# LoRA kernel on one core: A read as 128 rows of 4 KB in one transfer, its table columns put in place by the copies out of PSUM

## The chip, the cores and the metric

The kernel runs on one core of one Trainium2 chip. The metric is the device time in microseconds; the time of the kernel before is the median of three runs, 93.06 us (93.05 to 93.09).

## What is computed

Each of 64 sequences (64 tokens of 1024 features, float32) names one of 8 adapters of rank 16. The low-rank product of that adapter is added to the sequence:

```python
B_sel = B[adapter_ids]                       # B: [8, 16, 1024]
A_sel = A[adapter_ids]                       # A: [8, 1024, 16]
Bx = jnp.einsum('bni,bri->bnr', x, B_sel)
out = jnp.einsum('bnr,bor->bno', Bx, A_sel)
x = x + out * SCALING                        # SCALING = 1
```

x is 16 MB in and 16 MB out; A and B are 512 KB each.

## The kernel before

**Tiling.** x is 32 tiles of 128 tokens (two sequences each), all of which fit in SBUF (`x_all`). Two tiles make a duo, and the steady loop goes over 16 duos. For each duo TensorE transposes the eight 128x128 blocks of each tile (L217), multiplies them with the rank rows of B (`down`, L228) and, one duo later, multiplies the small result with the columns of A (`up`, L248). ScalarE copies the transposed x out of PSUM (`copy_x`, L301) and makes the high part of the small result (L316, L283); VectorE makes the remaining part (L352) and adds the product onto x (`add_x`, L361). GpSimd fetches the rows of the adapter that each sequence names from `b_table` (L156) and `a_table` (L166).

**Setup.** Before that the two tables are made. B is loaded by ScalarE's queue and transposed (L192), and two ScalarE copies write `b_table` (L293). A is loaded by SP's queue in two transfers of 256 KB, four adapters each. Partition p gets 8 successive outputs of each adapter, which are 512 contiguous bytes in HBM. A is split into a part that holds the high bits and a rest, in four pairs of adapters: ScalarE casts (L289), VectorE subtracts (L340). TensorE then transposes one adapter in four matmuls (`a_unit`, L206), each of which writes every fourth column of half a PSUM tile, so that the columns come out in order and a plain 512-element copy moves one adapter into `a_table`: six of the eight copies are VectorE's (L345), units 5 and 7 are ScalarE's (L306). The units take turns in four PSUM banks, so units 4 to 7 wait for the copies of units 0 to 3. TensorE runs 21 warm-up transposes on the identity first (L187). Its order is then: B, A units 0 to 3, the transposes of tile 0, A units 4 and 5, the transposes of tile 1, A units 6 and 7, the loop.

**Transfers.** SP issues, in this order on one queue: the A transfers, 17 loads of x (two of 512 KB, 15 of 1 MB), then the 32 stores of 512 KB, each when `add_x` of its tile is done. The loads that overwrite the place of A and its parts (tiles 26 to 31) wait for `a_filled`. Nothing but the last wait reads `stored`.

Of the kernel before, what the change touches and what calls it, by code (L numbers as in the profile page):

```python
# [8 lines left out]
def lora_kernel(nc: bass.Bass, x: bass.AP, ids: bass.AP, a_in: bass.AP, b_in: bass.AP, out: bass.AP):  # L9
# [5 lines left out]
    P = 128  # L15
# [16 lines left out]
    B_HOME, A_HOME, PARTS_HOME = TILES - 1, TILES - 2, TILES - 6  # L32
    B_OWN = CHUNKS * RANK
    WARM_UPS = 21
    GROUP = ADAPTERS // 2
    PAIR = 2
    PAIRS = ADAPTERS // PAIR

    rows = x.rearrange("s t d -> (s t) d").rearrange("(n p) d -> p n d", p=P)
    out_rows = out.rearrange("s t d -> (s t) d").rearrange("(n p) d -> p n d", p=P)  # L40
# [5 lines left out]
    with ctx:  # L46
# [6 lines left out]
        def sem(name):  # L53
# [10 lines left out]
        a_duo = [sb(f"a_duo{i}", [P, DUO_SEQS, BANK], F32R) for i in range(2)]  # L64

        b_nat = x_all[:, B_HOME, :]
        a_nat = x_all[:, A_HOME, :].rearrange("p (a o) -> p a o", a=ADAPTERS)
        a_parts = (x_all[:, PARTS_HOME:A_HOME, :].rearrange("p n d -> p (n d)")
                   .rearrange("p (a j k) -> p a j k", a=ADAPTERS, j=J))

        t_bank = [pb(f"t_bank{i}", [P, BANK]) for i in range(2)]
        bx_bank = [pb(f"bx_bank{i}", [P, BANK]) for i in range(2)]
        y_banks = [pb(f"y_banks{i}", [P, D]) for i in range(2)]

        ids_loaded = sem("ids_loaded")
        a_loaded = [sem(f"a_loaded{g}") for g in range(2)]
        b_loaded = sem("b_loaded")
        x_loaded = [sem(f"x_loaded{n}") for n in range(len(LOADS))]
        stored = sem("stored")
# [21 lines left out]
            half = a % A_BANKS // 2  # L101
            return y_banks[a % 2][:, half * BANK:(half + 1) * BANK]

        def a_raw(pair):
            raw = a_nat[:, pair * PAIR:(pair + 1) * PAIR, :].rearrange("p a (o r) -> p (a o) r", r=RANK)
            return raw.unsqueeze(2).to_broadcast([P, PAIR * J * HALVES, 2, RANK])

        def a_part(pair, part):
            both = (a_parts[:, pair * PAIR:(pair + 1) * PAIR, :, :]
                    .rearrange("p a j (h e t r) -> p (a j h) e t r", h=HALVES, e=2, t=2))  # L110
            return both[:, :, :, part, :]

        def a_row(a):
            return a_table[:, a * BANK:(a + 1) * BANK]

        def own_tokens(duo, first_row, end_row):
            blocks = (bx_parts[duo % 2][first_row:end_row, :, :]
# [2 lines left out]

        @block.sync
        def _(sp):
            for g in range(2):
                of = slice(g * GROUP, (g + 1) * GROUP)
                sp.dma_start(a_nat[:, of, :],
                             a_in.rearrange("a (p o) r -> p a (o r)", p=P)[:, of, :]).then_inc(a_loaded[g], 16)
            for n, (first, end) in enumerate(LOADS):
                if end > PARTS_HOME:
                    sp.wait_ge(a_filled, ADAPTERS)
                sp.dma_start(x_all[:, first:end, :], rows[:, first:end, :]).then_inc(x_loaded[n], 16)  # L130
            for tile in range(TILES):
                sp.wait_ge(y_drained, tile + 1)
                sp.dma_start(out_rows[:, tile, :], x_all[:, tile, :]).then_inc(stored, 16)
            sp.wait_ge(stored, 16 * TILES)
# [48 lines left out]
        @block.tensor  # L183
        def _(pe):
            pe.wait_ge(ident_steps, 2)
            for _ in range(WARM_UPS):
                nc.tensor.transpose(t_bank[0][:, 0:P], ident[:, :], ident[:, :])  # L187

            pe.wait_ge(b_loaded, 16)
            for unit in range(B_UNITS):  # L190
                for c in range(HALF):
                    last = nc.tensor.transpose(bx_bank[unit][:, c * P:(c + 1) * P],  # L192
                                               b_nat[:, (unit * HALF + c) * P:(unit * HALF + c + 1) * P], ident[:, :])
                last.then_inc(t_filled, 1)

            def a_unit(a):
                if a % PAIR == 0:
                    pe.wait_ge(a_rest_done, a // PAIR + 1)
                before = a - A_BANKS
                if before in A_BY_ACT:  # L200
                    pe.wait_ge(a_copied_act, A_BY_ACT.index(before) + 1)
                if before in A_BY_DVE:
                    pe.wait_ge(a_copied_dve, A_BY_DVE.index(before) + 1)
                filled = a_bank(a).rearrange("k (p j) -> k p j", j=J)
                for j in range(J):
                    last = nc.tensor.transpose(filled[:, :, j], a_parts[:, a, j, :], ident[:, :])  # L206
                last.then_inc(a_filled, 1)

            def transpose_unit(duo, unit):
                tile, half = unit // 2, unit % 2  # L210
                if unit == 0 or duo == 0 and half == 0:
                    pe.wait_ge(x_loaded[LOAD_OF[2 * duo + tile]], 16)
                if duo or unit >= 2:
                    pe.wait_ge(t_copied, B_UNITS + UNITS * duo + unit - 1)
                for c in range(HALF):
                    at = (half * HALF + c) * P
                    last = nc.tensor.transpose(t_bank[unit % 2][:, c * P:(c + 1) * P],  # L217
                                               x_all[:, 2 * duo + tile, at:at + P], ident[:, :])
                last.then_inc(t_filled, 1)

            def down(duo, first, end):
                if first == 0:
                    pe.wait_ge(b_gathered, duo + 1)
                pe.wait_ge(t_copied, B_UNITS + UNITS * duo + (3 if end <= HALF else 4))
                for c in range(first, end):
                    for k in range(DUO_SEQS):
                        tile, s = k // PER_TILE, k % PER_TILE
                        last = nc.tensor.matmul(bx_bank[duo % 2][k * QUAD:(k + 1) * QUAD, 0:SEQ],  # L228
                                                b_duo[duo % 2][:, k, c, :],
                                                x_t[duo % 2][:, c, tile, s * SEQ:(s + 1) * SEQ],  # L230
                                                start=(c == 0), stop=(c == CHUNKS - 1))
                if end == CHUNKS:
                    last.then_inc(bx_done, 1)

            def up(duo):
                pe.wait_ge(a_gathered, duo + 1)
                pe.wait_ge(parts_done, duo + 1)
                for tile in range(2):
                    if duo == 0:
                        pe.wait_ge(a_copied_act, len(A_BY_ACT))  # L240
                        pe.wait_ge(a_copied_dve, len(A_BY_DVE))
                    else:
                        pe.wait_ge(y_drained, 2 * (duo - 1) + tile + 1)
                    for s in range(PER_TILE):
                        for h in range(HALVES):
                            ranks = slice(h * K_UP, (h + 1) * K_UP)
                            k = tile * PER_TILE + s
                            last = nc.tensor.matmul(y_banks[tile][:, h * BANK:(h + 1) * BANK],  # L248
                                                    bx_parts[duo % 2][ranks, k, :], a_duo[duo % 2][ranks, k, :],
                                                    start=(s == 0), stop=(s == PER_TILE - 1))  # L250
                    last.then_inc(y_filled, 1)

            for a in range(A_BANKS):
                a_unit(a)
            transpose_unit(0, 0)
            transpose_unit(0, 1)
            a_unit(A_BANKS)
            a_unit(A_BANKS + 1)
            transpose_unit(0, 2)
            transpose_unit(0, 3)  # L260
            a_unit(A_BANKS + 2)
            a_unit(A_BANKS + 3)
            for duo in range(DUOS):
                if duo + 1 < DUOS:
                    transpose_unit(duo + 1, 0)
                    transpose_unit(duo + 1, 1)
                down(duo, 0, HALF)
                if duo + 1 < DUOS:
                    transpose_unit(duo + 1, 2)
                    transpose_unit(duo + 1, 3)  # L270
                down(duo, HALF, CHUNKS)
                if duo:
                    up(duo - 1)
            up(DUOS - 1)

        @block.scalar
        def _(act):
# [5 lines left out]
                nc.scalar.copy(own_tokens(duo, K_UP, 2 * K_UP),  # L283
                               own_tokens(duo, 0, K_UP)).then_inc(parts_done, 1)

            for pair in range(PAIRS):
                if pair % 2 == 0:
                    act.wait_ge(a_loaded[pair // 2], 16)
                nc.scalar.copy(a_part(pair, 0).bitcast(F32R), a_raw(pair)).then_inc(a_high_done, 1)  # L289

            for unit in range(B_UNITS):
                act.wait_ge(t_filled, unit + 1)
# [10 lines left out]

            def copy_a(a):
                act.wait_ge(a_filled, a + 1)
                nc.scalar.copy(a_row(a), a_bank(a)).then_inc(a_copied_act, 1)  # L306

            def split_high(duo):
                act.wait_ge(bx_done, duo + 1)
# [25 lines left out]

        @block.vector
        def _(dve):
            for pair in range(PAIRS):
                dve.wait_ge(a_high_done, pair + 1)
                nc.vector.tensor_tensor(a_part(pair, 1).bitcast(F32R), a_raw(pair), a_part(pair, 0),  # L340
                                        ALU.subtract).then_inc(a_rest_done, 1)

            for a in A_BY_DVE:
                dve.wait_ge(a_filled, a + 1)
                nc.vector.tensor_copy(a_row(a), a_bank(a)).then_inc(a_copied_dve, 1)  # L345

            def split_rest(duo):
                dve.wait_ge(high_done, duo + 1)
# [37 lines left out]
```

## Time and profile before

| | |
|---|---|
| median of 3 runs | 93.06 us |
| the profiled execution | 93.04 us, of which the span from the first to the last instruction is 91.2 us |
| TensorE busy (matmul / weight load) | 80.1 / 63.0 us |
| VectorE, ScalarE, GpSimd busy | 59.7, 59.0, 60.3 us |
| moved by DMA | 34.82 MB, mean 382 GB/s |
| mean granted TensorE clock | 0.961 |

In the profile "PE" is TensorE's matmuls, "PEld" its weight loads, DVE is VectorE, ACT ScalarE, POOL GpSimd. "L206" is line 206 of the kernel, shown above. A DMA share of 1.0 means that all 16 DMA engines of the core are moving packets; 0.06 is one of them.

### The profile page before, as it was taken

The numbers are of one execution on the slowest core, as the hardware profiler recorded it, in microseconds if no ns is written. First come the engines' busy times: TensorE is split into PE (matmuls) and PEld (weight loads), VectorE is DVE, ScalarE is ACT, GpSimd is POOL, SyncE is SP. The second block draws the span as 40 slices with busy tenths as digits, with TensorE's granted clock in tenths as the row PEclk, the third lists the DMA queues.
The fourth block names the chain that finished last, engine by engine and source line by source line (L and its number), as shares of the span: only waits on it lengthen the run. The fifth ranks groups of instructions, "written<-read, shape, count | busy, mean of one in ns | idle before, by whom it ended". The sixth has DMA issues, their size and how long they took to land.

```text
span 91.2 us, 3627 instructions
## 1 busy us (share of the span) xinstructions
PE 80.1 (88%) x1469; PEld 63.0 (69%) x1469; DVE 59.7 (65%) x106; ACT 59.0 (65%) x153; POOL 60.3 (66%) x136
## 2 busy tenths in 40 slices
PE   3999999999999999899999999999999999464400
PEld 3999988778687778587778687878787786322100
DVE  0039930359686768775959586776869696999900
ACT  1367698969696859396869596969695958131000
POOL 6000859999879697877878879797979793900000
PEclk9999999999999999999999999999999999999555
DMA  1899999999999999999999999999999999988890
GB/s 25 311 386 410 408 410 412 401 413 410 395 413 408 404 412 403 406 412 403 410 412 404 415 419 408 412 415 410 422 408 413 430 397 421 392 345 356 341 386 20
DMA packets 10193, 34.82 MB, mean 382 GB/s; under 512 B 834, under 2 KB 1858, under 8 KB 10178
## 3 DMA queue, kind: packets, MB, share of 16 engines
q1 hardware_dynamic: 10032, 34.08, 93.7%
q10 hardware_dynamic: 146, 0.52, 1.5%
q8 instruction: 11, 0.18, 0.8%
q14 instruction: 4, 0.03, 0.1%
HBM read 17.83 MB, written 16.78 MB: 380 GB/s over the span
## 4 chain that ended last, share of the span: by engine, by line
PE 85%; DVE 6%; issue 1%; ACT 1%; POOL 1%; POOLq 0%
PE t_bank L217 36%; PE y_banks L248 20%; PE bx_bank L228 20%; PE t_bank L187 5%; DVE x_all L361 4%; PE y_banks L206 4%; DVE bx_parts L352 2%; PE bx_bank L192 1%; ACT bx_parts L283 1%; POOL ident L140 0%; POOL ident L138 0%; POOLq L140 0%; POOLq L377 0%
## 5 line engine op out<-in xcount | busy, mean ns | idle before, releaser
L361 DVE TENSOR_TENSOR x_all<-y_banks,x_all 128x1024 f32<-128x1024 f32 x32 | 39.4, 1232 | 15.7 <-PE y_banks L248 15.1
L301 ACT COPY x_t<-t_bank 128x512 f32<-128x512 f32 x64 | 34.5, 592 | 13.9 <-PE t_bank L217 13.3
L166 POOL CAST a_duo<-a_table 128x512 fp32r x64 | 36.7, 615 | 3.1 <-PE y_banks L248 2.1
L217 PE MATMUL t_bank<-ident,x_all 128*128 128x128 f32 x256 | 34.9, 279 | 0.0
L156 POOL COPY b_duo<-b_table 128x256 f32 x64 | 22.8, 401 | 15.8 <-PE bx_bank L228 8.7
L217 PEld LDWEIGHTS t_bank<-ident,x_all 128*128 128x128 f32 x256 | 27.5, 141 | 7.0 <-issue 5.4
L248 PE MATMUL y_banks<-a_duo,bx_parts 64*128 64x512 f32 x128 | 20.6, 429 | 3.6 <-ACT bx_parts L283 3.2
L228 PE MATMUL bx_bank<-x_t,b_duo 128*32 128x64 f32 x1024 | 21.3, 222 | 0.0
L228 PEld LDWEIGHTS bx_bank<-x_t,b_duo 128*32 128x32 f32 x1024 | 16.1, 109 | 5.6 <-issue 5.2
L352 DVE TENSOR_TENSOR bx_parts<-bx_bank,bx_parts 32x64 fp32r<-32x64 f32 x64 | 14.1, 220 | 4.8 <-ACT bx_parts L316 3.7
L248 PEld LDWEIGHTS y_banks<-a_duo,bx_parts 64*128 64x128 f32 x128 | 10.9, 188 | 7.3 <-issue 3.8
L316 ACT CAST bx_parts<-bx_bank 32x64 fp32r<-32x64 f32 x64 | 13.1, 205 | 0.9 <-PE bx_bank L228 0.2
L283 ACT CAST bx_parts<-bx_parts 64x256 fp32r<-64x256 f32 x16 | 6.5, 405 | 5.3 <-DVE bx_parts L352 4.2
L340 DVE TENSOR_TENSOR x_all<-x_all 128x512 fp32r<-128x512 f32 x4 | 2.5, 688 | 6.0 <-ACT x_all L289 6.0
L187 PE MATMUL t_bank<-ident 128*128 128x128 f32 x21 | 4.4, 404 | 1.5 <-POOL ident L140 1.5
L187 PEld LDWEIGHTS t_bank<-ident 128*128 128x128 f32 x21 | 4.2, 221 | 1.5 <-POOL ident L140 1.5
L206 PE MATMUL y_banks<-ident,x_all 128*128 128x128 f32 x32 | 4.0, 274 | 0.0
L345 DVE CAST a_table<-y_banks 128x512 fp32r<-128x512 f32 x6 | 3.8, 685 | 0.3 <-PE y_banks L206 0.3
L206 PEld LDWEIGHTS y_banks<-ident,x_all 128*128 128x128 f32 x32 | 3.5, 140 | 0.2 <-DVE x_all L340 0.2
L289 ACT CAST x_all<-x_all 128x512 fp32r<-128x512 f32 x4 | 2.2, 616 | 2.2 <-DMA x_all<-in_A 2.2
L289 ACT ACT_TABLE_LOAD x1 | 1.3, 1283 | 1.9 <-issue 1.9
L306 ACT CAST a_table<-y_banks 128x512 fp32r<-128x512 f32 x2 | 1.1, 612 | 0.0
(10 smaller groups left out, 4.9 us busy)
## 6 DMA issues: line engine op xcount, KB each, us to landing
out_y<-x_all SPq DMA_DIRECT2D x32, 512.0 KB, 13.2
x_all<-in_x SPq DMA_DIRECT2D x15, 1024.0 KB, 19.0
x_all<-in_x SPq DMA_DIRECT2D x2, 512.0 KB, 6.1
x_all<-in_B ACTq DMA_DIRECT2D x1, 512.0 KB, 4.3
x_all<-in_A SPq DMA_DIRECT2D x2, 256.0 KB, 4.8
id_row<-in_ids ACTq DMA_DIRECT2D x1, 0.2 KB
```

Source lines behind the costliest of these rows:

```text
L156: last = nc.gpsimd.tensor_copy(b_duo[duo % 2][:, k, :, :].rearrange("p c (e r) -> p c e r", e=2), b_table[:, bass.ds(adapters[k] * B_OWN, ...
L166: last = nc.gpsimd.tensor_copy(a_duo[duo % 2][:, k, :], a_table[:, bass.ds(adapters[k] * BANK, BANK)])
L187: nc.tensor.transpose(t_bank[0][:, 0:P], ident[:, :], ident[:, :])
L206: last = nc.tensor.transpose(filled[:, :, j], a_parts[:, a, j, :], ident[:, :])
L217: last = nc.tensor.transpose(t_bank[unit % 2][:, c * P:(c + 1) * P], x_all[:, 2 * duo + tile, at:at + P], ident[:, :])
L228: last = nc.tensor.matmul(bx_bank[duo % 2][k * QUAD:(k + 1) * QUAD, 0:SEQ], b_duo[duo % 2][:, k, c, :], x_t[duo % 2][:, c, tile, s * SEQ:( ...
L248: last = nc.tensor.matmul(y_banks[tile][:, h * BANK:(h + 1) * BANK], bx_parts[duo % 2][ranks, k, :], a_duo[duo % 2][ranks, k, :], start=(s ...
L283: nc.scalar.copy(own_tokens(duo, K_UP, 2 * K_UP), own_tokens(duo, 0, K_UP)).then_inc(parts_done, 1)
L301: nc.scalar.copy(x_t[duo % 2][:, half * HALF:(half + 1) * HALF, tile, :], t_bank[unit % 2][:, :].rearrange("p (c n) -> p c n", c=HALF)).th ...
L316: last = nc.scalar.copy(bx_parts[duo % 2][0:QUAD, k, s * SEQ:(s + 1) * SEQ], bx_bank[duo % 2][k * QUAD:(k + 1) * QUAD, 0:SEQ])
L352: last = nc.vector.tensor_tensor(bx_parts[duo % 2][QUAD:K_UP, k, cols], bx_bank[duo % 2][k * QUAD:(k + 1) * QUAD, 0:SEQ], bx_parts[duo % 2 ...
L361: nc.vector.tensor_tensor(here, product, here, ALU.add).then_inc(y_drained, 1)
```

## The change

A is read in one transfer of 128 rows of 4 KB: partition 16a + b holds outputs 64b to 64b + 63 of adapter a. The split into the two parts keeps its four instructions on each engine (now over quarters of the row). A transpose of 128 columns now gives one pair of outputs (l of 0 to 31) for all adapters and blocks, and writes 128 neighbouring PSUM columns. Each of the eight copies out of PSUM still moves 512 elements on each of 128 partitions, but reads four columns that stand 128 apart (512 bytes) and writes them as a run of four (16 bytes), with 128 such runs, one in every 32 columns of `a_table`. The table's content is as before. The core of the diff:

```diff
         def _(sp):
-            for g in range(2):
-                of = slice(g * GROUP, (g + 1) * GROUP)
-                sp.dma_start(a_nat[:, of, :],
-                             a_in.rearrange("a (p o) r -> p a (o r)", p=P)[:, of, :]).then_inc(a_loaded[g], 16)
+            sp.dma_start(a_nat, a_in.rearrange("a (b o) r -> (a b) (o r)", b=BLOCKS)).then_inc(a_loaded, 16)
...
-                filled = a_bank(a).rearrange("k (p j) -> k p j", j=J)
                 for j in range(J):
-                    last = nc.tensor.transpose(filled[:, :, j], a_parts[:, a, j, :], ident[:, :])
+                    last = nc.tensor.transpose(a_bank(a)[:, j * P:(j + 1) * P], a_parts[:, a * J + j, :], ident[:, :])
...
-            for pair in range(PAIRS):
-                if pair % 2 == 0:
-                    act.wait_ge(a_loaded[pair // 2], 16)
-                nc.scalar.copy(a_part(pair, 0).bitcast(F32R), a_raw(pair)).then_inc(a_high_done, 1)
+            for quarter in range(QUARTERS):
+                if quarter == 0:
+                    act.wait_ge(a_loaded, 16)
+                nc.scalar.copy(a_part(quarter, 0).bitcast(F32R), a_raw(quarter)).then_inc(a_high_done, 1)
...
-        def a_row(a):
-            return a_table[:, a * BANK:(a + 1) * BANK]
+        def a_columns(u):
+            return (a_table[:, :].rearrange("k (a b l) -> k a b l", a=ADAPTERS, b=BLOCKS)
+                    [:, :, :, u * J:(u + 1) * J])
+
+        def a_filled_columns(u):
+            return a_bank(u).rearrange("k (l a b) -> k a b l", l=J, a=ADAPTERS)
...
-                nc.scalar.copy(a_row(a), a_bank(a)).then_inc(a_copied_act, 1)
+                nc.scalar.copy(a_columns(a), a_filled_columns(a)).then_inc(a_copied_act, 1)
...
-                nc.vector.tensor_copy(a_row(a), a_bank(a)).then_inc(a_copied_dve, 1)
+                nc.vector.tensor_copy(a_columns(a), a_filled_columns(a)).then_inc(a_copied_dve, 1)
```

## Rows read from the trace of the kernel before

**Rows 1.** The page: span, the two DMA rows of the 40 slices, the chain by line.

```profile
span 91.2 us, 3627 instructions
...
DMA  1899999999999999999999999999999999988890
GB/s 25 311 386 410 408 410 412 401 413 410 395 413 408 404 412 403 406 412 403 410 412 404 415 419 408 412 415 410 422 408 413 430 397 421 392 345 356 341 386 20
...
PE t_bank L217 36%; PE y_banks L248 20%; PE bx_bank L228 20%; PE t_bank L187 5%; DVE x_all L361 4%; PE y_banks L206 4%; DVE bx_parts L352 2%; PE bx_bank L192 1%; ACT bx_parts L283 1%; POOL ident L140 0%; POOL ident L138 0%; POOLq L140 0%; P
```

**Rows 2.** Busy time by engine, clock and DMA in stretches of the end.

```profile
48.50:77.00 28.50, 28.50 (x586) 22.27 (x576) 21.60 (x39) 22.33 (x61) 23.27 (x51) 1.00 1.03 414
...
80.70:81.40 0.70, 0.62 (x4) 0.18 (x4) 0.70 (x1) 0.00 (x0) 0.00 (x0) 1.00 0.62 252
...
84.10:84.80 0.70, 0.70 (x4) 0.47 (x4) 0.70 (x1) 0.00 (x0) 0.00 (x0) 0.50 0.24 99
85.00:88.70 3.70, 0.29 (x2) 0.00 (x0) 1.51 (x2) 0.00 (x0) 0.00 (x0) 0.50 1.01 411
88.90:89.10 0.20, 0.00 (x0) 0.00 (x0) 0.00 (x0) 0.00 (x0) 0.00 (x0) 0.50 0.21 82
89.30:90.30 1.00, 0.00 (x0) 0.00 (x0) 0.00 (x0) 0.00 (x0) 0.00 (x0) 0.50 0.06 25
```

**Rows 3.** Line L133: the last store (issued at 86.6 us), and all stores.

```profile
L133 SPq DMA_DIRECT2D out_y<-x_all x1: 332/332/332, 86.6 to 86.6; - x1
DMA to landing us min/median/max: 4.2/4.2/4.2
...
L133 SPq DMA_DIRECT2D out_y<-x_all x32: 332/383/2969, 32.8 to 86.6; - x32
DMA to landing us min/median/max: 3.8/13.2/16.5
```

**Rows 4.** DMA queues over the whole span: packets, MB, share.

```profile
q8 instruction: 11, 0.18, 0.8%
```

**Rows 5.** Timeline of the setup: start, us, engine, line, tiles.

```profile
0.74 0.99 SPq L125 DMA_DIRECT2D x_all<-in_A  x2
...
5.38 2.18 ACT L289 CAST x_all<-x_all 128x512 fp32r<-128x512 f32 x4 [2.22 <-DMA x_all<-in_A]
5.68 0.90 PEld L192 LDWEIGHTS bx_bank<-ident,x_all 128*128 128x128 f32 x8
...
6.78 1.73 PEld L206 LDWEIGHTS y_banks<-ident,x_all 128*128 128x128 f32 x16 [0.20 <-DVE x_all L340]
...
8.45 3.08 DVE L345 CAST a_table<-y_banks 128x512 fp32r<-128x512 f32 x5
...
11.10 0.90 PEld L206 LDWEIGHTS y_banks<-ident,x_all 128*128 128x128 f32 x8
...
12.88 1.12 ACT L301 COPY x_t<-t_bank 128x512 f32<-128x512 f32 x2
...
13.63 0.86 PEld L217 LDWEIGHTS t_bank<-ident,x_all 128*128 128x128 f32 x8
```

**Rows 6.** Busy time by engine, clock, DMA share and GB/s in stretches of the start.

```profile
1.80:2.50 0.70, 0.70 (x5) 0.70 (x5) 0.00 (x0) 0.63 (x1) 0.60 (x2) 1.00 0.41 97
2.50:3.00 0.50, 0.50 (x4) 0.50 (x3) 0.00 (x0) 0.50 (x1) 0.00 (x0) 1.00 0.68 242
3.00:4.00 1.00, 1.00 (x7) 1.00 (x6) 0.00 (x0) 0.15 (x1) 0.00 (x0) 1.00 1.03 400
4.00:5.00 1.00, 1.00 (x7) 1.00 (x6) 0.00 (x0) 0.00 (x0) 0.00 (x0) 1.00 1.04 331
5.00:5.60 0.60, 0.60 (x5) 0.60 (x5) 0.00 (x0) 0.22 (x1) 0.00 (x0) 1.00 1.28 399
5.60:15.00 9.40, 9.40 (x132) 8.78 (x134) 6.18 (x10) 7.83 (x16) 4.61 (x12) 1.00 1.02 408
```

**Rows 7.** DMA queues in the stretch 3.5 to 4.4 us: q1 is SP's, q10 ACT's.

```profile
q10 hardware_dynamic: 76, 0.26, 72.2%
q1 hardware_dynamic: 149, 0.08, 27.9%
```

**Rows 8.** Groups by line and shape: busy, mean ns of one, idle before.

```profile
L361 DVE TENSOR_TENSOR x_all<-y_banks,x_all 128x1024 f32<-128x1024 f32 x32 | 39.4, 1232 | 15.7 <-PE y_banks L248 15.1
...
L217 PE MATMUL t_bank<-ident,x_all 128*128 128x128 f32 x256 | 34.9, 279 | 0.0
...
L206 PE MATMUL y_banks<-ident,x_all 128*128 128x128 f32 x32 | 4.0, 274 | 0.0
L345 DVE CAST a_table<-y_banks 128x512 fp32r<-128x512 f32 x6 | 3.8, 685 | 0.3 <-PE y_banks L206 0.3
...
L306 ACT CAST a_table<-y_banks 128x512 fp32r<-128x512 f32 x2 | 1.1, 612 | 0.0
```

More of the change, by code:

```diff
@@ L34, in lora_kernel @@
     WARM_UPS = 21
-    GROUP = ADAPTERS // 2
-    PAIR = 2
-    PAIRS = ADAPTERS // PAIR
+    BLOCKS = P // ADAPTERS
+    A_UNITS = 8
+    QUARTERS = 4
+    PER_QUARTER = A_UNITS * J // QUARTERS
     rows = x.rearrange("s t d -> (s t) d").rearrange("(n p) d -> p n d", p=P)
@@ L66, in lora_kernel @@
         b_nat = x_all[:, B_HOME, :]
-        a_nat = x_all[:, A_HOME, :].rearrange("p (a o) -> p a o", a=ADAPTERS)
+        a_nat = x_all[:, A_HOME, :]
         a_parts = (x_all[:, PARTS_HOME:A_HOME, :].rearrange("p n d -> p (n d)")
-                   .rearrange("p (a j k) -> p a j k", a=ADAPTERS, j=J))
+                   .rearrange("p (l k) -> p l k", k=P))
         t_bank = [pb(f"t_bank{i}", [P, BANK]) for i in range(2)]
@@ L75, in lora_kernel @@
         ids_loaded = sem("ids_loaded")
-        a_loaded = [sem(f"a_loaded{g}") for g in range(2)]
+        a_loaded = sem("a_loaded")
         b_loaded = sem("b_loaded")
@@ L102, in a_bank, with a_raw, a_part @@
             return y_banks[a % 2][:, half * BANK:(half + 1) * BANK]
[L104 to L110, printed above, removed]
-            return both[:, :, :, part, :]
-        def a_row(a):
-            return a_table[:, a * BANK:(a + 1) * BANK]
+        def a_raw(quarter):
+            size = PER_QUARTER * HALVES
+            raw = a_nat[:, quarter * size * RANK:(quarter + 1) * size * RANK].rearrange("p (o r) -> p o r", r=RANK)
+            return raw.unsqueeze(2).to_broadcast([P, size, 2, RANK])
+        def a_part(quarter, part):
+            both = (a_parts[:, quarter * PER_QUARTER:(quarter + 1) * PER_QUARTER, :]
+                    .rearrange("p l (h e t r) -> p (l h) e t r", h=HALVES, e=2, t=2))
+            return both[:, :, :, part, :]
+        def a_columns(u):
[3 more added lines that the diff above has]
+            return a_bank(u).rearrange("k (l a b) -> k a b l", l=J, a=ADAPTERS)
         def own_tokens(duo, first_row, end_row):
@@ L122, in _ @@
         def _(sp):
-            for g in range(2):
-                of = slice(g * GROUP, (g + 1) * GROUP)
-                sp.dma_start(a_nat[:, of, :],
-                             a_in.rearrange("a (p o) r -> p a (o r)", p=P)[:, of, :]).then_inc(a_loaded[g], 16)
+            sp.dma_start(a_nat, a_in.rearrange("a (b o) r -> (a b) (o r)", b=BLOCKS)).then_inc(a_loaded, 16)
             for n, (first, end) in enumerate(LOADS):
                 if end > PARTS_HOME:
-                    sp.wait_ge(a_filled, ADAPTERS)
+                    sp.wait_ge(a_filled, A_UNITS)
                 sp.dma_start(x_all[:, first:end, :], rows[:, first:end, :]).then_inc(x_loaded[n], 16)
@@ L196, in a_unit @@
             def a_unit(a):
-                if a % PAIR == 0:
-                    pe.wait_ge(a_rest_done, a // PAIR + 1)
+                if a % 2 == 0:
+                    pe.wait_ge(a_rest_done, a // 2 + 1)
                 before = a - A_BANKS
@@ L337, in _ @@
         def _(dve):
-            for pair in range(PAIRS):
-                dve.wait_ge(a_high_done, pair + 1)
-                nc.vector.tensor_tensor(a_part(pair, 1).bitcast(F32R), a_raw(pair), a_part(pair, 0),
+            for quarter in range(QUARTERS):
+                dve.wait_ge(a_high_done, quarter + 1)
+                nc.vector.tensor_tensor(a_part(quarter, 1).bitcast(F32R), a_raw(quarter), a_part(quarter, 0),
                                         ALU.subtract).then_inc(a_rest_done, 1)
```

## The prediction

> **What bounds the kernel now.** I read the page first [rows 1]. The chain that ended last lies almost wholly on TensorE: three groups of the loop hold 76% of the span, and there is hardly a gap in it. Read alone, this says that whatever TensorE gains or loses at the start is gained or lost at the end. But the DMA rows of the same page stand at 9 in nearly every slice at about 410 GB/s, so there are two candidates, and the end has to be looked at by itself.
>
> The stretches of the end [rows 2] decide between them. From 48.5 to 77 us all 16 DMA engines are busy (share 1.03, 414 GB/s). At 80.7 the share falls to 0.62 and at 84.1 to 0.24: some engines have run out of stores to move and wait for VectorE's next tile, but about four of sixteen have not; they are behind. From 85.0 to 88.7 all are busy again with the last three stores. At 89.0 the share is 0.21, and from 89.3 to 90.3 it is 0.06 at 25 GB/s: a single DMA engine is moving the last packets, alone. The last store was issued at 86.6 and landed 4.2 us later, at 90.8 [rows 3]; the other engines had finished theirs some 1.5 us earlier.
>
> How long has that engine been behind? A packet of 4 KB at 25 GB/s takes 0.16 us, and a store is 128 packets, eight for each engine, 1.28 us. The three stores issued from 84.0 on hold 24 packets for each. From 84.1 to 90.3 an engine that never rests moves about 39. So the last engine, if it never rested, carried about 15 packets, two stores, that were older than 84 us, which fits with its being one of the four that were busy then. In the rows I find no point at which it can have run dry. What put it behind may be the eleven transfers of instructions, 16 KB each (0.18 MB in 11 packets) [rows 4], each of which one engine has to carry beside its share; that part is a guess. What matters is the reading: the end is set by one DMA engine that is busy from about 1.85 us to 90.3, and TensorE's chain has about 1.5 us of slack behind it. The stores have a backlog (13.2 us from issue to landing in the median, 3.8 at best) [rows 3], because all loads stand ahead of them in the queue. So the question is how much time the change takes out of the DMA stream, and only then what it does to TensorE.
>
> **The change, part by part.**
>
> (1) *DMA at the start, on the path.* Every packet of A and B stands ahead of x in the same 16 engines. The rate of the steady stage is 408 GB/s. Against it the stretches before 5.6 us fall short [rows 6]: 1.8 to 2.5 by 0.70 x (1 - 97/408) = 0.53 us; 2.5 to 3.0 by 0.20; 3.0 to 4.0 by 0.02; 4.0 to 5.0 by 0.19; 5.0 to 5.6 by 0.01. The sum is 0.95 us. The 0.19 lies where almost only A's 512-byte packets run (331 GB/s), and 4 KB rows should remove it whole: that is the low bound. The first two, 0.73 us, are the start, where A's short packets run alone and B's come in late; B moves at full rate as soon as it is there (400 GB/s). Some ramp stays: at 84.8 to 85.0 the engines go from a share of 0.24 to full within 0.2 us, so no more than about 0.2 us of 0.73 has to be lost. High bound: 0.19 + 0.5 + 0.02 + 0.01 = about 0.7, or 0.95 if nothing were lost. As the first packets of a cold start are slower than those of the tail, I take between half and three quarters of the 0.73, 0.42 us: together 0.6 us by which the whole stream of loads and stores moves forward. Bounds 0.2 and 0.95.
>
> The Trainium skill, DMA: Bandwidth & Descriptors, Specifications, names 512 bytes as the smallest transfer for line rate. By that rule packets of 512 bytes lose nothing and the 0.19 us would be nil; the stretch at 331 GB/s against 408 speaks against it. I keep it as a rival.
>
> (2) *A and B share alike.* While both queues had work, B's 4 KB packets took 0.26 MB against 0.08 MB of A [rows 7]: the engines alternate packets, not bytes. With equal packets A and B finish together, A earlier and B later than now. 1 MB at 408 GB/s is 2.57 us; from 1.85 plus 0.2 to 0.4 of ramp, the last packet is read at 4.6 to 4.8, and x shares a little with B's end. With half a microsecond of landing (the difference between 90.3, the last packet, and 90.8) A lands at 4.7 to 5.2, not 5.38 when its first half let ScalarE begin [rows 5], and B at 5.2 to 5.4. TensorE reaches B at 5.68, after its warm-ups, so B stays covered with 0.3 us left. If that cover were gone, TensorE would wait by as much, inside the slack.
>
> (3) *The 0.20 us wait.* TensorE waited 0.20 us for the first subtraction before A unit 0 [rows 5]. With A 0.2 us or more earlier this wait goes; next it would be B, which is covered. Gain on TensorE's chain 0.2, at the end nil.
>
> (4) *Splits and transposes.* The same four instructions on each of two engines and the same 32 transposes. Writing every fourth column costs nothing now: 274 ns against 279 for neighbouring columns [rows 8]. So 0.
>
> (5) *The copies.* Eight copies of 512 elements keep their count, but read at a step of 512 bytes and write runs of 16 bytes. Before shows no such pattern. Nearest row: `add_x` reads both operands at a step of 8 bytes, 1024 elements in 1232 ns; the plain copy takes 685 for 512 [rows 8]. The difference, 547 ns for 512 more elements, is the full rate of the plain copy or better, so a step alone costs VectorE nothing. Low bound 0; for the high bound I double the copy, at which each element would cost two steps. Cover: VectorE's copies follow one another at 0.62 us from 8.45, and unit 7 is filled from 11.5 on, when four copies have to be done. Four at D each: 8.45 + 4D against 11.5 allows D = 0.76. ScalarE's two copies stand just ahead of `copy_x` of duo 1: its first copy ends at 13.47 and TensorE wants it at 13.63, so 0.16 us is covered there. Above that TensorE is late by 4D - 3.05 plus 2(D - 0.62) - 0.16, that is 6D - 4.45: 0.15 us at 25% more, 1.7 at D = 1.03, 3.7 at D = 1.36. Behind these copies wait GpSimd's first fetch of A rows and `up` of duo 0; they shift with it. The first 1.7 us are hidden by the slack of the store stream, less what (1) takes of it. I take 0.
>
> (6) *SP.* One issue of A fewer, about 0.5 us of SP time; the x load behind it moves up, but its data waits for the engines. 0. The wait for `a_filled` stands ahead of loads that the queue reaches much later. 0.
>
> Sum: profiled execution 93.04 (span 91.2 and 1.84 around it) - 0.6 = 92.44; from the median 93.06, 92.46. Slack check: TensorE's side ends at about 89.3 minus 0.2, the late engine at 90.8 - 0.6 = 90.2, so it is still the last.
>
> **The rivals.** (A) TensorE's chain sets the end, and the late engine is an effect of it. For: the chain of the page. Against: one engine alone for a microsecond. Then only (3) counts: 92.86. 10%. (B) The DMA start gives nothing: 512-byte packets are at line rate and the slow ramp is latency. For: the ramp has few packets of any kind. Against: 331 GB/s in a full stretch. 93.0 to 93.1. 11%. (C) The copies are the cost: reading PSUM at 512 bytes is slow. It decides above 65% more per copy; at twice the time TensorE is late by 3.7 us, of which the slack takes 1.7: about 95.0. For: no row has this step. Against: the 8-byte step of `add_x` at full rate. 9%. The Trainium skill, SBUF — State Buffer, Door 1, says that non-contiguous PSUM access slows matmuls much, through lines of 8 bytes; line L206 against L217 does not show it. (D) The late engine is another one or is late by another amount, since what puts it behind falls differently: up to 1.3 us (one store) either way, 91.2 to 93.7. 8%, half each way. The forecast itself: 62%, 92.1 to 92.85.
>
> **The numbers.** What a measurement here can tell from no change is 0.2%, 0.19 us. Faster: 0.62 + 0.07 of A + 0.04 = 0.73. Slower: 0.09 + 0.04 = 0.13. Same: 0.14. The range takes in the forecast's own, A and the larger part of B: 92.05 to 93.05.
>
> **What would show it.** Right: the stretch 1.8 to 5 us above 350 GB/s; x tile 0 landing 0.6 us earlier and every load after it; L345 near 685 and L306 near 612 ns; no wait before L206; one DMA engine alone at the end, 0.6 us earlier. Wrong: L345 above 1000 ns, or A landing earlier while the late engine ends at the same moment.

## The result, and the profile after

The changed kernel takes 92.7 us (median of 22 runs, 92.33 to 93.11 without one at 113.85 us, whose mean granted clock was 0.66) against 93.08 for the kernel before in as many runs (92.85 to 93.26). The ratio of the means is 0.9956 with a 95% interval of 0.9947 to 0.9965: 0.41 us faster; the medians differ by 0.38. The prediction was 92.46. A ratio in this document leaves out executions over 1.5% longer than the fastest of the same kernel, which is the one of 113.85 us here and, in three experiments below, executions that are told there.

The page of the changed kernel: span, slices, instruction transfers, the chain by line and two groups.

```profile
span 90.9 us, 3626 instructions
...
DMA  2899999999999999999999999999999999869692
GB/s 29 355 409 417 420 409 411 400 411 411 398 413 402 409 411 402 398 411 409 402 411 404 418 417 409 413 422 409 413 415 413 418 404 411 350 276 409 267 406 112
...
q8 instruction: 11, 0.18, 0.8%
...
PE t_bank L219 36%; PE bx_bank L230 20%; PE y_banks L250 19%; PE t_bank L190 5%; DVE x_all L363 4%; PE y_banks L208 4%; DVE bx_parts L354 2%; DVEq L47 1%; PE bx_bank L195 1%; ACT bx_parts L285 1%; POOL ident L143 0%; POOL ident L141 0%; POOLq L143 0%; POOLq L379 0%
...
L347 DVE CAST a_table<-y_banks 128x512 fp32r<-128x512 f32 x6 | 3.8, 682 | 0.4 <-PE y_banks L208 0.4
```

The chain by line is within 1% of the span of the one before at every group shown [rows 1], and the spreading copies take 682 ns on VectorE, where plain ones took 685 [rows 8]. Nothing on this page says where 0.4 us went. The setup of the changed kernel in the timeline:

```profile
0.74 0.38 SPq L129 DMA_DIRECT2D x_all<-in_A  x1
...
1.52 4.34 PEld L190 LDWEIGHTS t_bank<-ident 128*128 128x128 f32 x21 [1.52 <-POOL ident L143]
...
5.58 2.18 ACT L291 CAST x_all<-x_all 128x512 fp32r<-128x512 f32 x4 [2.55 <-DMA x_all<-in_A]
5.85 1.20 PEld L195 LDWEIGHTS bx_bank<-ident,x_all 128*128 128x128 f32 x8
...
7.02 1.78 PEld L208 LDWEIGHTS y_banks<-ident,x_all 128*128 128x128 f32 x16
...
8.65 3.07 DVE L347 CAST a_table<-y_banks 128x512 fp32r<-128x512 f32 x5
```

A lets ScalarE begin at 5.58, 0.2 us *later* than before [rows 5]. TensorE no longer waits for the first subtraction, yet starts A at 7.02 instead of 6.78, since the same 29 transposes ahead of it took longer in this execution: the eight of B need 1.20 us where they needed 0.90. The line of B's eight weight loads shows why (number, then the shortest, the median and the longest in ns):

```profile
L195 PEld LDWEIGHTS bx_bank<-ident,x_all x8: 140/142/230, 5.8 to 6.9; 128*128 128x128 f32 x8
```

The weight loads of this part run at 230 ns each up to one moment and at about 140 ns from then on, while the granted clock reads 1.00 throughout. In the kernel before that moment came at 5.4 us, during the warm-ups; here it came at 6.5, within B. Over the fourteen profiled executions of this document it lies between 4.1 and 7.5 us, and what sets it is not shown. Every step of the compute chain is 0.2 to 0.3 us later than before, and VectorE's last result comes at 86.87 (84.51 + 2.36) where it came at 86.56. The time fell all the same. Stretches of the changed kernel at the start and the end (columns as in rows 2):

```profile
1.80:2.50 0.70, 0.70 (x5) 0.70 (x5) 0.00 (x0) 0.70 (x1) 0.60 (x2) 1.00 0.55 117
2.50:3.00 0.50, 0.50 (x4) 0.50 (x3) 0.00 (x0) 0.50 (x1) 0.00 (x0) 1.00 0.73 262
3.00:4.00 1.00, 1.00 (x7) 1.00 (x6) 0.00 (x0) 0.03 (x1) 0.00 (x0) 1.00 1.01 414
4.00:5.00 1.00, 1.00 (x7) 1.00 (x6) 0.00 (x0) 0.00 (x0) 0.00 (x0) 1.00 1.04 414
5.00:5.60 0.60, 0.60 (x4) 0.60 (x4) 0.00 (x0) 0.02 (x1) 0.00 (x0) 1.00 0.99 383
5.60:15.00 9.40, 9.40 (x112) 8.97 (x114) 6.18 (x10) 7.74 (x15) 4.34 (x11) 1.00 1.03 416
...
85.00:85.30 0.30, 0.30 (x4) 0.00 (x0) 0.30 (x1) 0.00 (x0) 0.00 (x0) 0.50 0.07 27
85.50:89.20 3.70, 0.00 (x0) 0.00 (x0) 1.36 (x2) 0.00 (x0) 0.00 (x0) 0.50 1.00 402
89.40:90.00 0.60, 0.00 (x0) 0.00 (x0) 0.00 (x0) 0.00 (x0) 0.00 (x0) 0.50 0.05 20
```

Between 4 and 5 us the engines move 414 GB/s, not 331 [rows 6]; before 3 us hardly more than before. The end has the picture of before with less to spare: a single engine works while the others wait for VectorE (share 0.07 at 85.0), where about four did before (0.24 at 84.1), and one works alone after 89.4. The line of the wait that ends the kernel, SP's for the last landing, is the best single measure:

```profile
SPq L47 <- DMA out_y<-x_all: 3.3, 1, 3.3
```

It was 3.9 in the kernel before (its line was L46). From issue to landing the last store took 3.6 us instead of 4.2.

### The profile page after: what moved, and what is told of

Same layout as the page of the kernel before. It is cut to its first block, busy times and chain, and to the rows that moved or that the text cites. A ratio compares the mean times of both kernels' runs of the same rounds, so it can differ in the third digit from the quotient of the medians.

```text
span 90.9 us, 3626 instructions
## 1 busy us (share of the span) xinstructions
PE 79.8 (88%) x1469; PEld 63.1 (69%) x1469; DVE 59.6 (66%) x106; ACT 59.0 (65%) x153; POOL 60.6 (67%) x136
## 4 chain that ended last, share of the span: by engine, by line
PE 84%; DVE 6%; issue 2%; DVEq 1%; ACT 1%; POOL 1%; POOLq 0%
PE t_bank L219 36%; PE bx_bank L230 20%; PE y_banks L250 19%; PE t_bank L190 5%; DVE x_all L363 4%; PE y_banks L208 4%; DVE bx_parts L354 2%; DVEq L47 1%; PE bx_bank L195 1%; ACT bx_parts L285 1%; POOL ident L143 0%; POOL ident L141 0%; POOLq L143 0%; POOLq L379 0%
## 5 line engine op out<-in xcount | busy, mean ns | idle before, releaser
L195 PE MATMUL bx_bank<-ident,x_all 128*128 128x128 f32 x8 | 1.2, 302 | 0.0
```

## The experiments

All ratios are to the kernel before, run on the same chip.

**The new load alone.** The kernel before, with A as 4 KB rows; ScalarE's first cast now waits for the whole of A.

```diff
-            for g in range(2):
-                of = slice(g * GROUP, (g + 1) * GROUP)
-                sp.dma_start(a_nat[:, of, :], ...).then_inc(a_loaded[g], 16)
+            sp.dma_start(x_all[:, A_HOME, :],
+                         a_in.rearrange("a (b o) r -> (a b) (o r)", b=16)).then_inc(a_loaded[0], 16)
```

> The kernel before with the new load alone: A as 128 rows of 4 KB in one transfer, everything behind it unchanged, so the adapters' columns are mixed up in the table (the output is another one; the work is the same). Theory (the end is set by the DMA stream, and the change shortens its start by about 0.45 us): x tile 0 lands about 0.45 us earlier than in the kernel before and the time is that of the change, ratio 0.995 to 0.997. Rival (TensorE's chain sets the end and the gain came from the new transposes and copies): ratio 1.000 or above, since A lands 0.2 us later.

Measured: 0.9965 (0.9953 to 0.9978), 92.68 us. The load alone brings what the change brings, within the two intervals. x tile 0 lands at 7.1 us here and at 7.0 in the change, 5.9 us after an issue at 1.2; before it was 7.5 (1.8 + 5.7). In the nine profiled executions that load A in long rows beside B and have x right behind it, this landing lies between 6.89 and 7.16; with short packets in two transfers it was 7.49 in the kernel before and 8.14 in the run "The new compute alone" below.

**One transfer, short packets.** The kernel before, its two transfers of A merged; the first cast waits for the whole of A here too.

```diff
+            sp.dma_start(a_nat[:, :, :],
+                         a_in.rearrange("a (p o) r -> p a (o r)", p=P)).then_inc(a_loaded[0], 16)
```

> The kernel before with its two 256 KB transfers of A merged into one of 512 KB that keeps the 512-byte packets. Theory (the size of the packets is what shortens the stream): ratio 1.000, x tile 0 lands within 0.1 us of the kernel before. Rival (one issue fewer, so x follows sooner): ratio 0.996 and x tile 0 about 0.4 us earlier.

Measured: 1.005 (1.002 to 1.008), 93.56 us. Neither expectation held; the merging itself costs. x tile 0 lands at 7.8 (1.2 + 6.6), 0.3 us later than before, and TensorE waits for the first subtraction. The stretches of this kernel's start:

```profile
1.80:2.50 0.70, 0.70 (x5) 0.70 (x5) 0.00 (x0) 0.55 (x1) 0.59 (x2) 1.00 0.35 80
2.50:3.00 0.50, 0.50 (x4) 0.50 (x3) 0.00 (x0) 0.50 (x1) 0.00 (x0) 1.00 0.62 102
3.00:4.00 1.00, 1.00 (x7) 1.00 (x6) 0.00 (x0) 0.23 (x1) 0.00 (x0) 1.00 1.04 388
```

and its wait, where before had 0.2:

```profile
PEld y_banks L204 <- DVE x_all L338: 0.9, 1, 0.9
```

102 GB/s between 2.5 and 3.0, against 242 before: B's packets came in later still. Why is open. So the gain is not that of one transfer fewer; it needs the long rows.

**The new compute alone.** The changed kernel with the old load; one wait for both halves (32 on the semaphore).

```diff
+            for g in range(2):
+                of = slice(g * 4, (g + 1) * 4)
+                sp.dma_start(nat[:, of, :],
+                             a_in.rearrange("a (p o) r -> p a (o r)", p=P)[:, of, :]).then_inc(a_loaded, 16)
```

> The changed kernel with A loaded as in the kernel before (two transfers, 512-byte packets; the columns are mixed up in the table), so that only the transposes into neighbouring columns and the spreading copies are new. Theory: ratio 1.000 (within 0.1%), copies 682 and 611 ns. Rival: the compute part carries the gain, 0.996.

Measured: 1.0019 (1.0005 to 1.0032), 93.11 us; the copies take 683 and 610 ns. No gain in the compute part. The interval leaves out 1.000 narrowly; the first cast here waits for the second half of A (6.36 us), which the kernel before did not do, and x tile 0 landed at 8.1 in the profiled execution, 0.6 us later than in the kernel before.

**TensorE later by nine warm-ups.**

```diff
-    WARM_UPS = 21
+    WARM_UPS = 30
```

> The changed kernel with 30 warm-up transposes instead of 21: nine more, so that all of TensorE's chain is 1.0 us (at 0.11 us each) to 2.0 us (at 0.22 us each) later, while the DMA stream is untouched. Theory (TensorE's chain has about 1.2 us of slack behind the late DMA engine): the end moves by 0 to 0.3 us for 1.0 us of delay, ratio 0.996 to 0.999. Rival (TensorE's chain sets the end): 1.0 us or more later than the change, ratio 1.006 or above.

Measured: median 92.86 us, ratio 1.0007 (0.9982 to 1.0032), the runs from 92.69 to 93.68. In the profiled execution VectorE ends at 87.37, only 0.5 us later than in the change although nine transposes were put in, because the weight loads went from 230 to 140 ns already at 4.6 us; the last landing moves by 0.1, as a slack of 0.8 us asks. The ratio lies just above the range of the theory and below that of the rival: against the change the mean is 0.4 us longer, where 0 to 0.3 and 1.0 or more were expected. Eight of twelve runs lie below 93.1, four between 93.4 and 93.7.

**TensorE later by 27 warm-ups.**

```diff
-    WARM_UPS = 21
+    WARM_UPS = 48
```

> The changed kernel with 48 warm-up transposes, 27 more, which is 3.0 us of TensorE time at 0.11 us each (less by what the clock's rise gives back). In the change VectorE ends at 86.9 and the last landing is at 90.5; an undisturbed store needs 2.5 to 2.7 us after VectorE, so the slack is 0.9 to 1.1 us. Theory: the time rises by 3.0 - 1.0 = about 2.0 us over the change, ratio to the kernel before 1.015 to 1.022, and at the end the DMA engines finish within 0.5 us of one another. Rival (TensorE's chain alone): 3.0 us, ratio 1.028.

Measured: 95.06 us median of four runs (93.33, 94.27, 95.86 and 97.08), too wide for a ratio. The two long ones are longer than even the rival allowed (1.028 is 95.7), and what made them long is open. The profile, of the run of 94.27, says more. Its stretches from 82.5 us on, and its last wait:

```profile
82.50:85.00 2.50, 1.00 (x7) 0.30 (x4) 2.36 (x6) 0.30 (x2) 0.00 (x0) 1.00 0.67 267
...
86.00:89.00 3.00, 1.59 (x8) 0.60 (x5) 2.46 (x3) 0.00 (x0) 0.00 (x0) 0.50 0.55 221
89.00:91.40 2.40, 0.00 (x0) 0.00 (x0) 0.13 (x1) 0.00 (x0) 0.00 (x0) 0.50 1.01 408
91.50:91.90 0.40, 0.00 (x0) 0.00 (x0) 0.00 (x0) 0.00 (x0) 0.00 (x0) 0.50 0.01 0
```

```profile
SPq L47 <- DMA out_y<-x_all: 2.5, 1, 2.5
```

Now no engine is left alone at the end, and the wait is 2.5 us: that is a store with no backlog. So the slack is the last wait less 2.5: 3.9 - 2.5 = 1.4 us in the kernel before, 0.8 in the change. VectorE's end moved by 2.3 us against the change (89.13 to 86.87) and the last landing by 1.5 (91.9 to 90.5), as a slack of 0.8 asks.

**One store fewer.**

```diff
                 sp.wait_ge(y_drained, tile + 1)
+                if tile == 8:
+                    continue
```

> The changed kernel without the store of tile 8 (that tile of the output is not written), 1.28 us less for each DMA engine in the middle of the run; no computing engine is touched. Theory: the late engine gets free 1.28 us earlier until the slack of about 1.0 us is used up, so the time falls by 0.8 to 1.1 us against the change, ratio 0.983 to 0.988. Rival (TensorE's chain sets the end): no change against the changed kernel, 0.9956.

Measured: 0.9872 (0.9831 to 0.9914), some 0.8 us faster than the change, although no computing engine has less to do. That is from the four runs between 91.4 and 92.3; two more took 92.9 and 93.3, and over all six the mean is 92.2, 0.4 us below the change. The profile is of the run of 92.9: VectorE ended at 87.78, 0.9 us later than in the change, the last wait is 2.5 us, and the last landing comes at 90.6. So in this execution TensorE's chain sets the end and the missing store gains nothing.

**TensorE earlier by six warm-ups.**

```diff
-    WARM_UPS = 21
+    WARM_UPS = 15
```

> The changed kernel with 15 warm-up transposes instead of 21, which takes up to 1.3 us from the front of TensorE's chain (it then waits for B and A, which land at 5.5). Theory: no change against the changed kernel, 0.994 to 0.997. Rival (TensorE's chain sets the end): it gains what TensorE gains, some 0.3 us, 0.992, or loses if the clock rises later.

Measured: 0.9997 (0.9968 to 1.0025) without five runs between 93.88 and 94.08; over all twelve, from 92.33 to 94.08, the mean is 93.37, 0.7 us above the change. So no change against the changed kernel, which the theory asked for, is not what was found: fewer warm-ups make it slower. In the profiled execution (92.48) TensorE waits 1.2 us for B and 0.3 for the first subtraction, its weight loads go to 140 ns at 4.3 us, and nothing is gained. The long runs were not profiled, so what made them long is open; that TensorE gets to the shorter weight loads later there, which the expectation names, is not ruled out.

**Eight rows apart in the last two stores.**

```diff
+                for r0, r1 in ((0, 120), (120, P)):
+                    sp.dma_start(out_rows[r0:r1, tile, :], x_all[r0:r1, tile, :]).then_inc(stored, 16)
```

> The changed kernel with the last two stores each issued as 120 rows and 8 rows. Should a transfer of 120 rows go to 15 engines with 8 rows each, the sixteenth carries up to two stores fewer, and eight engines one row more per store. Theory, if the late engine is the one relieved: the time falls by 0.8 to 1.1 us, ratio 0.984 to 0.988. If another engine is the late one: the same as the change or 0.1 to 0.4 us slower, 0.996 to 1.000. If TensorE's chain sets the end: 0.1 to 0.4 us slower as well, since there is one more issue after VectorE's last result.

Measured: 1.0034 (1.0006 to 1.0063) without two runs at 94.39 and 94.86, slower than any of the three expectations. The last two tiles move at 164 GB/s (87 to 88 us) and 201 (88 to 89), where the change has 402, and there are two issues more, one of them behind VectorE's last result. The last of the landings (91.8) is only 0.2 us behind the one before it, so no engine is clearly the late one. How the rows were spread over the engines cannot be read from it, and it says nothing on the theory.

**Half of the product with B.**

```diff
-                for c in range(first, end):
+                for c in range(first, end, 2):
```

> The changed kernel with every second chunk left out of the product with B (half of the 1024 matmuls of that line; the output lacks half of the sum). TensorE needs 1.1 us less per duo; GpSimd, at about 4.0 us of fetches per duo against 4.34 for TensorE now, becomes the slowest engine, so VectorE's last result comes 3 to 5 us earlier, at 82 to 84. There are also 1024 instructions fewer on TensorE, which should be three or four instruction transfers fewer of the eleven. Theory (DMA stream): with the stores never short of work every engine runs through, and the last landing stays near 90.5 less 1.3 us for each instruction transfer that no longer falls on the late engine, so 88.0 to 90.5, a ratio of 0.970 to 0.995. Rival (TensorE's chain): 3 to 5 us less, ratio 0.945 to 0.965.

Measured: 0.9771 (0.9750 to 0.9792), 90.91 us (90.83 to 90.99). Its stretches at the end, its instruction transfers and its last wait:

```profile
77.00:80.00 3.00, 1.46 (x8) 0.58 (x4) 2.46 (x3) 0.00 (x0) 0.00 (x0) 0.50 1.02 416
80.00:84.00 4.00, 0.00 (x0) 0.00 (x0) 0.00 (x1) 0.00 (x0) 0.00 (x0) 0.50 1.03 420
84.00:86.00 2.00, 0.00 (x0) 0.00 (x0) 0.00 (x0) 0.00 (x0) 0.00 (x0) 0.50 0.99 404
86.00:88.00 2.00, 0.00 (x0) 0.00 (x0) 0.00 (x0) 0.00 (x0) 0.00 (x0) 0.50 0.37 152
87.00:88.50 1.50, 0.00 (x0) 0.00 (x0) 0.00 (x0) 0.00 (x0) 0.00 (x0) 0.50 0.09 36
```

```profile
q8 instruction: 7, 0.11, 0.5%
```

```profile
SPq L47 <- DMA out_y<-x_all: 8.2, 1, 8.2
```

VectorE is done at 80.0, 6.9 us earlier than in the change, and all computing engines stand still while the DMA engines work on at full rate for six microseconds; the first of them stop at 85.6, eight are left at 87, and one works until 88.2. The time falls by 1.8 us only. This is the DMA stream by itself, with four instruction transfers fewer.

**One load more.**

```diff
+        spare = sb("spare", [P, D])
...
+            sp.dma_start(spare[:, :], rows[:, 4, :]).then_inc(spare_loaded, 16)
```

> The changed kernel with one more 512 KB load in 4 KB packets (a tile of x into a spare buffer that nothing reads) between A and tile 0 of x. x tile 0 then lands at about 8.3 us, before TensorE asks for it at 8.8. Theory (DMA stream): 8 packets of 0.16 us more on every engine, 1.28 us, all of it at the end: ratio to the kernel before 1.008 to 1.011. Rival (TensorE's chain sets the end): no change against the changed kernel, 0.9956.

Measured: 1.008 (1.0064 to 1.0096), 93.82 us, and all six runs within 0.11 us. VectorE's last result comes at 86.6, 0.2 us *earlier* than in the change, and the kernel ends 1.1 us later, as eight packets of 0.16 us on each engine ask. The last wait:

```profile
SPq L141 <- DMA out_y<-x_all: 4.5, 1, 4.5
```

**B issued behind A on one queue.**

```diff
+            sp.dma_start(b_nat, b_in.rearrange("a r i -> (a r) i")).then_inc(b_loaded, 16)
...
-            act.dma_start(b_nat, b_in.rearrange("a r i -> (a r) i")).then_inc(b_loaded, 16)
```

> The changed kernel with B issued by SP right behind A instead of by ACT, so that A no longer shares the engines with B. The same bytes and packets stand ahead of x. Expected: A lands at 4.4 to 4.8 us instead of 5.5, B at 5.4 to 5.7, x tile 0 unchanged at 7.0. The first cast is no longer near TensorE's path. Theory (DMA stream): the same as the change within 0.2%, 0.993 to 0.998; a gain only in runs in which TensorE's chain is late. If A's landing mattered: 0.9 us less, 0.986.

Measured: 0.9970 (0.9943 to 0.9996), 92.62 us, as the change. Its timeline:

```profile
4.33 2.18 ACT L291 CAST x_all<-x_all 128x512 fp32r<-128x512 f32 x4 [1.77 <-DMA x_all<-in_A]
5.60 0.86 PEld L196 LDWEIGHTS bx_bank<-ident,x_all 128*128 128x128 f32 x8 [0.49 <-DMA x_all<-in_B]
```

A is there 1.25 us earlier than in the change, and it is worth nothing at the end that these seven runs could tell.

**Half of the product, with small matmuls as a filler.**

```diff
+                    for _ in range(32):
+                        last = nc.tensor.matmul(bx_bank[duo % 2][0:QUAD, BANK - 8:BANK], ident[:, 0:QUAD],
+                                                ident[:, 0:8], start=True, stop=True)
```

> The kernel with half of the product with B left out, and with 32 very small matmuls per duo put in (8 columns each, into PSUM columns that nothing reads), which bring TensorE's instruction count back to that of the change at little time. VectorE's last result should still be near 80 to 82 us, far ahead of the stores. Theory (the instruction transfers are what puts one DMA engine behind): about eleven of them again instead of seven, and the last landing goes from 88.7 back towards 90.5: ratio to the kernel before 0.988 to 0.996. Rival (the late engine has another cause, and the four transfers fewer were no part of the gain): as without them, 0.977.

Measured: 1.2278, 114.47 us. A failed experiment. The filler, counted as 64 matmuls per duo instead of 32, took TensorE 2.17 us per duo (34 ns each), so TensorE became the bound by far, and there were 15 instruction transfers. It says nothing on what the four transfers fewer were worth. That VectorE's last result (109.5) and the last landing (112.3) are again 2.8 us apart fits a kernel whose stores have no backlog.

## Why the prediction was right

**The bound.** Right, and shown from both sides. Taking 6.9 us from the compute chain (half of the product) gave 1.8 us and left a kernel that the stores alone end; adding 1.28 us per engine to the DMA stream cost 1.1 us while the compute chain was no later. The missing store agrees less firmly, with 0.8 us or 0.4 over all its runs. TensorE's 85% of the chain in the page is true and not the bound: the page's chain follows the instruction that was last, and the stores' backlog is not in it. Rival A falls with this, and rival B with the new load alone. Rival D, another late engine or another amount, can't be excluded for a few tenths: the last landing moved by 0.3 us where x tile 0 moved by 0.45.

**The slack.** Said to be 1.5 us, measured 1.4 in the kernel before. In the change 0.8 us is left, since its stream ends earlier and its compute chain was later in the profiled execution. The slack belongs to an execution and not to a kernel: by the same measure it is 0.5 us with the new load alone and 0.6 with the new compute alone, where the weight loads got shorter at 7.5 and 6.5 us. "TensorE's side ends at about 89.3 minus 0.2" was right in kind, but its 0.2 was not gained: TensorE's side was 0.3 us later.

**The DMA start, (1).** The mechanism was right, the size was not: 0.6 us said, 0.45 measured at x tile 0 (7.49 to 7.04, from the landings) and 0.3 at the last landing (90.8 to 90.5). The term at fault is the ramp. I took 0.42 us back from the stretches before 3 us. They went from 97 to 117 and from 242 to 262 GB/s, which is 14 + 10 KB, or 0.06 us at 410 GB/s. The tail's quick ramp was the wrong row for it: the start stays slow with long packets too. The stretches from 3 to 5 us gave (14 + 83) KB or 0.24 us, against the 0.19 + 0.02 said, and 5.0 to 5.6 took 0.02 back. That is 0.28 us. The rest of the shift lies where the prediction did not look: from 5.6 to 15 us the rate is 416 GB/s instead of 408, which is 75 KB or 0.18 us. So that the forecast came as near as it did is in part luck, for a ramp priced 0.36 too high was half made up by a term that was left out.

A plainer working was open in the trace of before. Between 4.4 and 5.0 us nearly all packets are A's short ones:

```profile
q1 hardware_dynamic: 412, 0.20, 112.9%
```

Some 400 packets of 512 bytes in 0.6 us on 16 engines are one in 24 ns for an engine, while a 4 KB packet takes 156 to 158. Each engine had 64 short packets of A (1.54 us) and has 8 long ones (1.26 us): an estimate of 0.3 us, with no ramp in it, against the 0.45 measured.

The Trainium skill, DMA: Bandwidth & Descriptors, Specifications, gives 512 bytes as the smallest transfer for line rate, and by that this term would be nil. The stretch from 4 to 5 us speaks against it: 331 GB/s with the short packets and 414 with the long ones, at an engine share of 1.04 in both.

**A and B, (2).** Half wrong. The two do share packet by packet, but A landed at 5.55 and B at 5.77 (0.74 + 4.8 and + 5.0), not at 4.7 to 5.2 and 5.2 to 5.4, which were built on the same ramp. The lower end for A did not even follow from its own working, which has the last packet read at 4.6 to 4.8 and half a microsecond of landing behind it. B issued behind A shows the sharing: without it A is there at 4.33. The cover of B was 0.08 us instead of 0.3, and that only because TensorE's warm-ups took longer; TensorE never waited for B in the profiled execution of the change and did with 15 warm-ups.

**The 0.20 us wait, (3).** It went, as said, but by TensorE being later and not by A being earlier. It was rightly priced at nothing.

**Transposes and copies, (4) and (5).** Right: 272 against 274 ns, 682 against 685, 611 against 612. Reading PSUM at a step of 512 bytes and writing runs of 16 bytes costs neither VectorE nor ScalarE anything here, and rival C falls. The ladder of delays in (5) mixes two bases (25% over 0.62 us is 0.775 and gives 0.20, not 0.15, while 1.36 is twice the 685 ns of the copy itself); nothing hung on it.

**Why engines are late.** The record says more on this than the experiments asked. Each load lands on 16 engines, and the trace has the 16 landings one by one. In the kernel before they lie within 0.46 us of one another for the seven transfers that land before 14 us. The first instruction transfer runs from 15.7 to 16.8 us, and of the load that lands next fifteen landings lie within 0.44 us and one comes 1.4 us behind them. The next packets of instructions start at 22.5 and 22.8, 28.6, 34.8 and 35.2, 41.6 and 45.7 us (those at 22.8, 34.8 and 45.7 are of 8 KB and on another queue), and the number of engines that are more than 0.6 us behind the first goes to three, four, six, seven and eight; the distance from first to last stays at 1.7 to 2.1 us. With half of the product the packets come at other times (16.0, 22.8, 26.7, 33.5 and 34.4, 42.3 and 42.4 us), and the count follows them: one, two, three, five and seven. So a packet of instructions does put an engine behind, as the prediction guessed, and up to 48 us each of them meets another engine instead of piling up on one.

**What is open.** How many of the transfers the last engine carried by the end. With 7 instruction transfers instead of 11 the last landing came 1.8 us earlier, which is consistent with one or two of them on that engine, but no landing after 48 us tells the engines apart, and the kernel that should have decided it failed. And the gain of 0.41 us lies between the 0.45 of the stream and the 0.3 of the two profiled ends; with a slack of 0.8 us or less, a late compute chain can eat part of it in single runs. The spreads fit that but do not prove it: 0.1 to 0.2 us in the two kernels whose stores have the most backlog (the extra load, half of the product), 0.4 to 1.0 in the sets of runs of the kernel before, 0.8 in the change, 1.9 without one store.

## What to carry to other kernels

When a kernel moves as much as its DMA engines can carry, read the last microseconds first: the DMA share slice by slice after the last issue, and the wait for the last landing less that of a store without backlog (2.5 us here), which is the slack of all computing. Then price an edit in packets taken out of the stream, not in instructions of the engine that the chain names; and expect the next gain of that kind to be smaller, since each one uses up the slack.

## What the runs showed of the hardware

Packets of 512 bytes and of 4 KB alternate one for one between two queues while both have work. Between 3 and 4 us of the kernel before (packets, MB, share):

```profile
q10 hardware_dynamic: 87, 0.36, 88.8%
q1 hardware_dynamic: 86, 0.04, 14.5%
```

So the queue with short packets gets a small share of the bytes. (In the stretch of [rows 7] the counts are 149 to 76, since part of the engines had no packets of B left at its end.)

Merging two transfers of short packets into one made the start worse (102 GB/s against 242 between 2.5 and 3.0 us, time up by 0.5%), which I had not expected; why is open.

An instruction transfer of 16 KB takes 0.9 to 1.2 us of one DMA engine. By the single landings of the loads one engine is then about 1.3 us behind the others, and up to 48 us each such packet adds one late engine (eight by 46.7 us in the kernel before, seven with half of the product), while the delay of the latest stays the same.

The same 21 warm-ups and eight transposes of B ran with weight loads of 0.90 us for the eight in one execution and 1.20 in another: single weight loads go from 230 to 140 ns at a moment that differs from one execution to the next (4.1 to 7.5 us), at a granted clock that reads 1.00 on both sides of it. In this kernel the slack behind the stores hides it, and a shorter DMA stream uncovers it.
